# Attention block on one core: maxima of two key chunks as b + relu(a - b) for eight units, and a new order of the work

## What is computed

```python
q, k, v = split(x @ W_qkv.T)                      # 16 heads, width 8
q, k = rope(q), rope(k)
scores = q @ k.T / sqrt(8)
scores = where(causal, scores, -inf)
attn = softmax(scores, axis=-1)
x = layernorm(x + (attn @ v) @ W_o.T)
x = layernorm(x + x @ int4_rounded(kernel) + bias + (x @ a) @ b)
```

## Time and profile before

| | |
|---|---|
| median of 3 runs | 437.37 us (437.16 to 437.58) |
| profiled execution | 437.25 us |
| its span, first to last instruction | 435.5 us |
| mean granted TensorE clock | 0.985 |
| TensorE, VectorE, ScalarE, POOL busy | 95%, 86%, 72%, 26% of the span |

### The profile page before, as it was taken

One profiled execution on the slowest core, in us unless ns is written; L12 is line 12 of the kernel. 1 busy time (PEld: TensorE's weight loads), 2 busy tenths in 40 slices (PEclk: granted clock), 3 DMA queues, 4 the chain that ended last, 5 costly groups with the idle time before them and its releaser, 6 DMA issues.

```text
span 435.5 us, 8512 instructions
## 1 busy us (share of the span) xinstructions
PE 412.0 (95%) x3250; PEld 202.5 (47%) x3250; DVE 374.5 (86%) x487; ACT 313.5 (72%) x552; POOL 114.6 (26%) x184
## 2 busy tenths in 40 slices
PE   5999799999999999999999999999999999999992
PEld 2556444354335453465453544444354354436651
DVE  2878889999999989998899999999989977657586
ACT  2454765785776877686877797978786888898761
POOL 8879610202212111212011213003003001205534
PEclk9999889999999999999999999999999999999997
DMA  7522322200000000022200022200000000000011
GB/s 236 187 99 78 133 65 69 74 25 3 0 2 3 2 2 4 2 70 60 75 3 2 6 81 62 59 2 2 2 2 2 2 2 2 3 2 3 3 50 49
DMA packets 12200, 16.57 MB, mean 38 GB/s; under 512 B 2444, under 2 KB 7324, under 8 KB 12160
## 3 DMA queue, kind: packets, MB, share of 16 engines
q1 hardware_dynamic: 11072, 15.75, 11.6%
q0 software_dynamic: 1088, 0.28, 0.4%
HBM read 10.37 MB, written 5.24 MB: 36 GB/s over the span
## 4 chain that ended last, share of the span: by engine, by line
PE 78%; DVE 15%; ACT 4%; issue 2%; DMA 1%; SPq 0%; DVEq 0%; ACTq 0%
PE ps L1296 28%; PE ps L1280 19%; PE ps L1227 17%; DVE pmax L1038 13%; PE ps L1195 3%; ACT probs L961 3%; PE ps L1305 2%; PE ps L1241 2%; PE ps L1237 1%; PE ps L1211 1%; PE ps L1324 1%; PE ps L1201 1%; DMA x_sb<-in_L_attn_x_dram 1%; PE ps L1251 1%; PE ps L1328 1%
## 5 line engine op out<-in xcount | busy, mean ns | idle before, releaser
L1038 DVE TENSOR_REDUCE pmax<-ps 128x2 f32<-128x1024 f32 (+3 forms) x273 | 318.4, 1214 | 35.3 <-PE ps L1227 20.0
L961 ACT ACTIVATE probs<-ps 128x512 f32<-128x512 f32 (+4 forms) x485 | 282.1, 655 | 81.9 <-PE ps L1280 80.8
L1280 PE MATMUL ps<-qS,kS 64*128 64x512 f32 (+3 forms) x664 | 149.9, 404 | 2.8 <-DVE pmax L1038 2.3
L1296 PE MATMUL ps<-probs,vP 128*9 128x512 f32 (+3 forms) x1328 | 146.4, 520 | 0.2
L1227 PE MATMUL ps<-kS,qS 64*128 64x512 f32 (+3 forms) x640 | 137.1, 418 | 6.6 <-DVE pmax L1038 2.3
L1280 PEld LDWEIGHTS ps<-qS,kS 64*128 64x128 f32 x664 | 78.4, 187 | 81.0 <-ACT probs L961 45.6
L1227 PEld LDWEIGHTS ps<-kS,qS 64*128 64x128 f32 x640 | 64.9, 186 | 68.5 <-DVE pmax L1038 29.1
L868 POOL TENSOR_SCALAR_AFFINE_SELECT probs<-probs 128x512 f32<-128x512 f32 x64 | 40.4, 635 | 123.3 <-ACT probs L961 123.2
L877 POOL DMA_DIRECT2D qS<-mrows x34 | 19.6, 578 | 163.5 <-DVE mrows L1058 163.5
L1296 PEld LDWEIGHTS ps<-probs,vP 128*9 128x9 f32 x1328 | 21.1, 88 | 39.2 <-issue 26.8
L1241 PEld LDWEIGHTS ps<-causal_x,ident_x 64*128 64x128 f32 x188 | 17.9, 186 | 0.0
(11 more groups left out here) (120 smaller groups left out, 188.5 us busy)
## 6 DMA issues: line engine op xcount, KB each, us to landing
qS<-q_parts SPq DMA_DIRECT2D x52, 64.0 KB
kS<-k_parts SPq DMA_DIRECT2D x52, 64.0 KB
cs<-rope_tables_dram SPq DMA_DIRECT2D x4, 512.0 KB, 6.7
q_parts<-qp SPq DMA_DIRECT2D x4, 512.0 KB, 2.8
k_parts<-kp SPq DMA_DIRECT2D x4, 512.0 KB, 2.8
x_sb<-in_L_attn_x_dram SPq DMA_DIRECT2D x4, 256.0 KB, 5.8
out_dram<-rot SPq DMA_DIRECT2D x2, 256.0 KB, 2.4
qS<-mrows POOLq DMA_DIRECT2D x30, 8.0 KB, 1.8
```

The lines of the kernel that those rows point to most:

```text
L961: nc.scalar.activation(probs[:, J % PRING, heads[0]:heads[-1] + 1:3 - len(banks), lo:hi], src, ACT.Exp, scale=float(DK) ** -0.5).then_inc( ...
L1038: nc.vector.tensor_reduce(dst, src, AX.X, ALU.max).then_inc(unit_free, 1)
L1280: last = nc.tensor.matmul(ps[:, bank, at:at + w], kS[rows, b, j // TPC, hp, (j % TPC) * TOK:(j % TPC + 1) * TOK], qS[rows, b, c, hp, lo:hi ...
L1296: last = nc.tensor.matmul(bank_of(("PV", n, 0))[VW * h:VW * h + VC, lo:hi], vP[:, j, HG * g + h, :], probs[:, J % PRING, h, lo:hi], start= ...
```

## The change

It touches group 0, chunk 2 (query tiles 1 and 3) and chunk 3 (query tiles 0 and 2). For each of these 4 tiles and both pairs of heads, the two units with key chunks 0 and 1 are replaced, so 16 plain units make room for 8 units "diff" and 8 units "pair":

- "diff": TensorE accumulates in the same two banks the product with key chunk 0 and the product with the negated key chunk 1, which gives a - b. ScalarE writes relu(a - b) into one of two buffers `folds`, which lie in `xT`, and frees the banks.
- "pair": TensorE computes b, the product with key chunk 1. VectorE adds relu(a - b) to b and keeps the maximum of the sum, max(a, b), per row: one `tensor_tensor_reduce` of 128 x 512 for each of the two heads. Both halves write one slot, that of key chunk 0.

ScalarE negates key chunk 1 of group 0 once, behind the projections of chunk 2 (`negate_keys`, 128 x 1024 values). `units` sets each "diff" two blocks of plain units ahead of its "pair"; the first unit of the tasks (0,2) and (0,3) is a "diff". In PROLOGUE the value projection of chunk 3 goes from ahead of the row selection of chunk 2 (E 2) to behind it.

TURNS is replaced as a whole; it holds as many letters of each kind as before (273 A, 394 S, 91 D, 166 V, ...). The last A has 548 score sets and 148 value steps ahead of it before, 546 and 149 now. The 90th A has 119 sets and 31 value steps ahead of it before, 124 and 32 now. Several constants of Course change too.

```diff
+PAIR_TILES = {(0, 2): (1, 3), (0, 3): (0, 2)}
+LEAD, FOLDS = 1, 2
 def units(n):
     g, c, first, end = TASKS[n]
-    return [("keys", kk, ii, hp) for kk in reversed(range(c)) for ii in range(first, end) for hp in range(PAIRS)] + list(OWN[first, end])
+    paired = [ii for ii in PAIR_TILES.get((g, c), ()) if first <= ii < end]
+    plain = [("keys", kk, ii, hp) for kk in reversed(range(c)) for ii in range(first, end) for hp in range(PAIRS) if kk >= 2 or ii not in paired]
+    plain += list(OWN[first, end])
+    pairs = [(ii, hp) for ii in paired for hp in range(PAIRS)]
+    out, last, rounds = [], plain.pop(), len(pairs) + LEAD
+    for i in range(rounds if pairs else 0):
+        out += [("diff", *x) for x in pairs[i:i + 1]]
+        out += plain[len(plain) * i // rounds:len(plain) * (i + 1) // rounds]
+        out += [("pair", *x) for x in pairs[i - LEAD:i - LEAD + 1] if i >= LEAD]
+    return (out if pairs else plain) + [last]
...
+    if unit[0] in ("diff", "pair"):
+        return [(unit[1], unit[2], kk, CH) for kk in ((0, "N") if unit[0] == "diff" else (1,))], None
...
-            (35.0, 1.9, "P", 3, 1), (35.0, 0, "R", 3, 1), (35.0, 1.1, "V", 1), (36.0, 0, "D", 2), (37.0, 1.1, "V", 2), (40.0, 1.1, "V", 3),
-            (44.0, 0.9, "E", 2, 0), (45.0, 0.9, "E", 2, 1), (45.0, 0, "H", 3, 0), (45.0, 0, "T", 3, 0), (48.0, 0, "H", 3, 1),
+            (35.0, 1.9, "P", 3, 1), (35.0, 0, "R", 3, 1), (35.0, 1.1, "V", 1), (36.0, 0, "D", 2), (37.0, 1.1, "V", 2),
+            (44.0, 0.9, "E", 2, 0), (45.0, 0.9, "E", 2, 1), (47.0, 1.1, "V", 3), (45.0, 0, "H", 3, 0), (45.0, 0, "T", 3, 0), (48.0, 0, "H", 3, 1),
...
+        folds = [xT[:, 2 * i:2 * i + 2, :] for i in range(FOLDS)]
...
+            def positive_part(n, unit):
+                e = ("A", n, unit)
+                at = DIFF[e]
+                act.wait_ge(unit_done, UNIT[e])
+                if at == 0:
+                    prep_freed(act, ("V", NC - 1))
+                if at >= FOLDS:
+                    released(act, FOLDED[at - FOLDS])
+                nc.scalar.activation(folds[at % FOLDS], unit_banks(e), ACT.Relu).then_inc(diff_done, 1)
+
+            def negate_keys():
+                prep_freed(act, ("E", 1, 1, PAIRS - 1))
+                nc.scalar.activation(kN[:, :, :], kS[:, 0, 1, :, :].bitcast(fp32), ACT.Copy, scale=-1.0).then_inc(negated, 1)
...
             for e in SCHEDULE:
+                if e[0] == "A" and e[2][0] == "diff":
+                    positive_part(*e[1:])
+                if e == ("X", 3):
+                    negate_keys()
...
                 dve.wait_ge(unit_done, UNIT[e])
+                if kind == "pair":
+                    at = FOLDED.index(e)
+                    dve.wait_ge(diff_done, at + 1)
+                    for hl in range(2):
+                        relu, slot = folds[at % FOLDS][:, hl, :], area + PLACE[first, end][unit[1]] * SLOTS + 3
+                        last = nc.vector.tensor_tensor_reduce(relu, src[:, hl, :], relu, 1.0, NEG, ALU.add, ALU.max, pmax[:, hl, unit[2], slot:slot + 1])
+                    last.then_inc(unit_free, 1)
+                    return
                 nc.vector.tensor_reduce(dst, src, AX.X, ALU.max).then_inc(unit_free, 1)
...
                         last = nc.tensor.matmul(ps[:, HELD[e][hl], at:at + w], qS[rows, b, c, hp, ii * TOK:(ii + 1) * TOK],
-                                                kS[rows, b, kk, hp, 0:w], start=i == 0, stop=masked is None and i == len(parts) - 1)
-                    at += w
+                                                kN[rows, hp, 0:w] if kk == "N" else kS[rows, b, kk, hp, 0:w],
+                                                start=i == 0, stop=masked is None and i == len(parts) - 1)
+                    at += w if unit[0] != "diff" else 0
```

More of the change, by code:

```diff
@@ L78, in mask_widths, with first_keys @@
     return [tiles * TOK, tiles * TOK // 2] if masked else []
+def first_keys(n, unit):
+    keys = [products(n, u)[0][0][2] for u in units(n)]
+    return keys.index(products(n, unit)[0][0][2]) == units(n).index(unit)
 def width(n, unit):
@@ L224, in operands @@
             return FAR if any(x[2] == "E" and x[3] <= c for x in PROLOGUE[self.p:]) else self.placed[c]
[L225 removed]
+        at = max(LOADED.index((g, x)) for x in (c, *(p[2] for p in products(n, unit)[0])) if (g, x) in LOADED)
         return self.arrived[at] if at < len(self.arrived) else FAR
@@ L472 @@
     last.update((b, e) for b in HELD.get(e, ()))
+DIFF = {e: i for i, e in enumerate(e for e in SCHEDULE if e[0] == "A" and e[2][0] == "diff")}
+FOLDED = [("A", e[1], ("pair", *e[2][1:])) for e in DIFF]
 STEP = {e[1:3]: i for i, e in enumerate(e for e in SCHEDULE if e[0] == "S" and e[3] == 0)}
@@ L1022, in row_max @@
                 src, kind, area = unit_banks(e), unit[0], AREA[n]
-                if unit == units(n)[0]:
+                if unit == next(u for u in units(n) if u[0] != "diff"):
                     dve.wait_ge(slots_set, 1)
@@ L1219, in scores @@
                     operands_in(pe, g, c)
-                if unit[0] == "keys" and unit[2:] == (first, 0):
-                    operands_in(pe, g, unit[1])
+                for _, _, kk, _ in parts:
+                    if kk == "N":
+                        pe.wait_ge(negated, 1)
+                if first_keys(n, unit):
+                    operands_in(pe, g, parts[0][2])
+                if unit[0] == "diff":
+                    operands_in(pe, g, 1)
                 banks_taken(pe, e)
```

66 lines of the change are left out of this document (49 added, 17 removed).

## The result

The changed kernel takes 440.06 us (median of 4 runs, 439.21 to 441.01) against 437.39 for the kernel before: a ratio of 1.0062, with a 95% interval from 1.0040 to 1.0084. It is slower by 2.7 us, where 4.2 less were forecast, and it lies above the range. The profiled execution is one of 439.8 us, with a span of 438.1, 2.6 more than before.

A forecast was written before the change was run, and what follows sets the result against it. VectorE was taken to bound 48 to 137 us: its 85.24 busy us become 78.1, at a 92% share 4.1 us less, other terms 0. So 437.25 - 4.1 = 433.1, or 433.2 for the median; range 428.8 to 438.8.

The forecast's parts named there:

- The order between 137 and 360 us is new, with the same work ... I take 0: New order of the work from 137 to 360 us: effect unknown in sign, taken as 0, 3 us either way.
- With 92% the stage takes 84.9 us, 4.1 less: Stage of 48 to 137 us: VectorE's 78.1 busy us at a 92% share take 84.9 us, saving 4.1.
- the sign of being wrong that the prediction had named: VectorE's idle time inside the 48 to 137 us stage above 8 us, with the Relus or TensorE as releaser.
- there VectorE sets the pace: From 58 to 137 us VectorE, busy 40.75 of 42 and 36.59 of 37 us, was taken as the limit.
- VectorE's saving: Eight pairs replacing 16 reductions of maxima: 0.89 us saved per pair on VectorE, 7.1 us in all.
- The negation at 0: ScalarE's 1.1 us negation ahead of chunk 3's input copy: cost 0, hidden by POOL's late start; 1.1 us without that cover.
- Products at 0 while VectorE sets the pace: Eight more pairs of 512-column products on TensorE, 1.9 us: cost 0 there, 1.9 if TensorE were the limit.
- The slower rival: Relus behind exponentials in ScalarE's queue hold two banks, VectorE runs dry once per pair: 440.4 us, chance 0.19.
- The hole at the lower clock: VectorE's hole of 1.86 us before 57.08 us, while TensorE has 1.2 GHz; more columns and moved values might fill it.
- the rival of full gain: VectorE stays at 95.8% and the new order loses nothing: gain 7.5, or 9.4 with the hole, 428 to 430; chance 0.16.
- The tail: Stretch from the last reduction at 402 us to the end of the span: 33.5 us, left unchanged.
- The accumulator read: Second VectorE instruction reading out each half-pair's maximum: 0.157 us, making a pair cost 1.50 and the saving 6.1 us.

The follow-up runs named there:

- z2_floor: Kernel before, VectorE's reductions of 56 units over other key chunks in tasks 2 to 4 cut to 256 of 512 columns per head: 431.70 us.
- w1_floor_after: Changed kernel, its 40 plain units over other key chunks in tasks 2 to 4 and 16 half-pair instructions cut to 256 of 512 columns: 439.09 us.
- x1_plain_in_place: Changed kernel, same order and PSUM banks, with plain units in place of differences and pairs and no Relu; negation stays: 446.32 us.
- x3_half_reduce: Kernel before, VectorE reducing only half of the columns in the 16 units that the change touches: 435.49 us.
- w2_floor_cheap: Changed kernel with VectorE's maxima cut as in w1_floor_after, only the first product of each difference, and negation behind the copy of chunk 1's values: 437.46 us.
- e4_late_negation: Changed kernel with the negation behind the copy of chunk 1's values, not ahead of the copy of chunk 3's transposed input: 439.10 us.
- y3_one_product: Changed kernel, each difference computing only its first product, with the negated keys left out: 439.58 us.
- x4_short_relu: Changed kernel, each Relu covering 64 of 512 columns per head: 440.23 us.
- x2_pairs_in_place: Kernel before, same order and PSUM banks, with differences and pairs in place of the 16 units, four buffers and the negation late: 439.94 us.
- z4_short_pairs: Changed kernel, each of the 16 half-pair instructions on VectorE over 256 of 512 columns: 439.60 us.
- z1_spread: Kernel before, VectorE's reductions of 56 units over other key chunks in tasks 2 to 4 cut to 439 of 512 columns per head: 433.87 us.

## Why the prediction was wrong

The traces, each from its first reduction on, give one account of the 2.1 us. Without VectorE's limit in tasks 2 to 4, the old list needs 409.7 us and the new one 416.4 (z2_floor, w1_floor_after). To this VectorE, with what the lower clock costs the kernel before, adds 5.9 there (415.5) and 1.3 in the changed one (417.6). So the pairs took 4.6 us off that, and the list that makes room for them is 6.7 us longer: 6.7 - 4.6 = 2.1 (differences from the unrounded times). It is one way to divide it. The other keeps VectorE's work whole: the new list with the old content takes 8.8 us more than the old one, and the pairs take 6.7 of them back (424.3 to 417.6, x1_plain_in_place; TensorE's clock falls in that run as in the kernel before, so the 6.7 have a share of the clock in them). In the old order a gift of VectorE time priced at 8.5 us was worth 1.9 (x3_half_reduce).

- **The step that failed: "The order between 137 and 360 us is new, with the same work ... I take 0", with 3 us either way.** With plain units in every place and no Relu the new list is 8.8 us longer than the old one (x1_plain_in_place), and with VectorE out of the way, no second products and the negation moved, 5.8 (w2_floor_cheap). Of these, 7.6 and 5.1 come by the fold of task 4, ahead of 137 us or close to it: in the very stage the sum was made for, and where it had no term for a new order. The bound was read from how VectorE's share varies between stages, so it couldn't show how TensorE and ScalarE fare in another order.
- **With it fell the step "With 92% the stage takes 84.9 us, 4.1 less".** From its first unit to its last the stage takes 86.8 us, 0.8 less than before, with VectorE busy for 77.25 of them (89%). Of its idle time 8.6 us lie ahead of the plain reductions, nearly all waiting for TensorE: that is the sign of being wrong that the prediction had named, idle time above 8 us with TensorE as releaser. Nor does the order keep scores and maxima "at the same ratio": at the 90th unit it has done 5 more score sets and one more value step.
- **The premise "there VectorE sets the pace" held only for 5.7 us**, the clock's part included. The share of 97% was true; it doesn't say how soon the next engine takes over. TensorE stood right behind, as its share of 78% in the chain said, which the prediction explained away. Of the chain between 58 and 100 us VectorE's reductions held 36.8% in the kernel before and 6.3% in z2_floor, and of what z2_floor gains only 2.1 us were won after 68 us; the rest comes in the first 20 us of the stage, where the clock of the kernel before is at its lower level for a time (0.66 in 48 to 58 us).
- **VectorE's saving**: 7.4 us measured in the stage for 7.1 forecast, and the prices of the pair were right. That it would be worth 4.1 us comes near the account above (4.6), but by luck: in the old order it would have been twice too much (x3_half_reduce), and with the old content as the measure the pairs are worth 6.7.
- **The negation at 0**: it cost about 0.4 us (e4_late_negation, by the trace; the medians are 1.0 apart). The step looked at POOL, which takes up the rotation late; but the copy that the negation delays feeds TensorE first (1.04 us of waiting at 33.08), and all maxima stand behind it in program order. The cover was there in part: of the 1.1 us without it, two thirds were hidden.
- **Products at 0 while VectorE sets the pace**: 0.5 to 0.7 us (y3_one_product).
- **The slower rival** foresaw the sign and nearly the time (440.4), but that is luck. In the changed kernel shorter Relus gain nothing (x4_short_relu), and a difference waits for its Relu for 0.3 us on average. Its mechanism shows in the old order (x2_pairs_in_place), which the change didn't use. In the first 10 us behind the prologue ScalarE is indeed what the chain waits for, but cutting the Relus alone didn't bring that back.
- **The hole at the lower clock** did go, as the rival of full gain said: the granted clock is 1.00 in 56 to 57 us, where it was 0.50.
- **The tail** behind the last reduction is 1.0 us shorter, for a forecast of no change.
- **The accumulator read** exists as the Trainium skill says ("VectorE: DVE Perf Modes", "Two Vector instructions with no wait between them"), and the trace agrees: 16 instructions of 83 ns. But the next half starts right when it does (both at 56.88), 0.61 us after the first half, so that a pair takes 1.30 us (56.27 to 57.57), not 1.50.

What stays open: by what the new list holds the engines up. Its cost is measured, but not which letters cost TensorE the 3.4 us between 70 us and the last maxima, nor how much of the 5.8 us comes of the Relus' places in ScalarE's queue. No full version tried was faster than the kernel before; the nearest, the changed kernel with the late negation, has 439.10.

## What to carry to other kernels

Before pricing a saving on the engine that looks full, ask how much the kernel would gain if that engine cost nothing there: one run with its instructions cut short answers it for the list as it stands, and here the answer was 5.7 us, little for a change that needed a new order of the whole work. Where several engines follow one fixed list, a new list is a cost of its own, to be measured with the old content in the new places and the new content in the old ones. A small instruction put into an in-order queue is free only if every reader of what stands behind it is late, not just the nearest one.

## What was not expected of the hardware

The rows before it don't tell when TensorE's clock falls to its lower level (1.2 of 2.4 GHz). Windows of 1 us, columns as in the earlier trace rows, of the changed kernel and then of z4_short_pairs:

```profile
51.00:52.00 1.00, 0.46 (x3) 0.30 (x3) 1.00 (x1) 1.00 (x2) 1.00 (x2) 1.00 0.00 0
54.00:55.00 1.00, 0.43 (x6) 0.42 (x6) 0.59 (x1) 1.00 (x3) 0.62 (x1) 1.00 1.02 377
56.00:57.00 1.00, 1.00 (x12) 0.30 (x4) 1.00 (x4) 0.96 (x2) 0.64 (x1) 1.00 0.40 148
```

```profile
53.00:54.00 1.00, 0.45 (x3) 0.19 (x2) 1.00 (x1) 1.00 (x3) 0.99 (x2) 1.00 1.01 358
54.00:55.00 1.00, 0.93 (x6) 0.93 (x8) 0.30 (x2) 1.00 (x3) 0.09 (x1) 0.62 0.94 318
55.00:56.00 1.00, 1.00 (x11) 0.69 (x11) 1.00 (x2) 0.97 (x3) 0.25 (x1) 0.50 0.42 99
```

The changed kernel sinks to 0.46 and 0.43 busy and keeps its clock (1.00); the other, with the same list and shorter pairs, sinks to 0.45 and falls to 0.50. Around it z4_short_pairs loses 1.5 us: its units are 0.5 us ahead of the changed kernel's up to the fall, 1.0 behind right after it, and 0.6 behind from 77 us to the end. The ten executions of w1_floor_after show the price within one kernel: 438.15 to 438.65 us at a mean granted clock of 0.997, 438.98 to 439.21 at 0.994, 439.48 to 439.87 at 0.991. So gains of 1 us around such a stretch are to be read from several runs (z1_spread's range goes from 432.57 to 436.43). The other source of scatter is the start: the first reduction comes between 19.60 and 20.75 us with the same work ahead of it, so two traces are to be laid over each other at an event behind the first loads, not at their first instruction.

A Relu out of PSUM costs what an exponential of the same shape costs, as the prediction had taken it: 1.034 us against 1.024 for 128x1024.
